# Keyed products and P times V one step further behind the scores in three 16-head attentions

## The reference, cut to what matters

```
scores = einsum('bhqd,bhkd->bhqk', q, k) * scale
scores = where(causal, scores (+ bias in layer 1), -inf)
attn = softmax(scores)
out = einsum('bhqk,bhkd->bhqd', attn, v) @ W_o
```

## Time and profile before

| | |
|---|---|
| median of 3 runs | 2973.53 us |
| lowest, highest | 2969.06, 2974.83 us |
| the profiled execution | 2965.65 us, its span 2963.8 us |
| PE busy | 2372.4 us (80%) |
| DVE, ACT, POOL busy | 1467.8 us (50%), 1140.7 us (38%), 637.5 us (22%) |
| granted clock, mean over the span | 0.898 |

### The profile page before, as it was taken

The page is one execution under the profiler, slowest core; times in us unless marked ns, Lnnn a source line. Parts: engine busy times, 40 slices in busy tenths (PEclk is TensorE's granted clock), DMA queues, the critical chain, the costliest instruction groups (busy, mean ns, idle before and its releaser), DMA issues. The chain is left out here.

```text
span 2963.8 us, 54617 instructions
## 1 busy us (share of the span) xinstructions
PE 2372.4 (80%) x19643; PEld 1552.7 (52%) x19644; DVE 1467.8 (50%) x3082; ACT 1140.7 (38%) x1810; POOL 637.5 (22%) x689
## 2 busy tenths in 40 slices
PE   5487999997799999785888458259997768999987
PEld 1133777773267777332555235135553315777764
DVE  4635666635466664445666123166663254554542
ACT  5623554523254444333555212225453421222223
POOL 0204443300344441011100320521110121211100
PEclk8797999998799999887999789579998867999997
DMA  2000000000000000002222311112220013332320
GB/s 106 0 0 1 1 1 0 0 1 0 0 1 1 0 0 1 1 4 61 76 71 61 144 47 35 46 54 67 72 69 2 32 39 96 99 91 91 91 73 29
DMA packets 81244, 115.93 MB, mean 39 GB/s; under 512 B 10352, under 2 KB 67184, under 8 KB 77720
## 3 DMA queue, kind: packets, MB, share of 16 engines
q1 hardware_dynamic: 79024, 109.35, 12.0%
q0 software_dynamic: 2048, 4.20, 0.5%
HBM read 69.57 MB, written 42.86 MB: 38 GB/s over the span
## 5 line engine op out<-in xcount | busy, mean ns | idle before, releaser
L1247 ACT ACTIVATE at_pr<-ps 128x768 f32<-128x768 f32 x384 | 312.1, 813 | 549.6 <-PE ps L1181 549.6
L1286 DVE TENSOR_REDUCE at_m<-ps 128x2 f32<-128x256 f32 x384 | 163.3, 425 | 424.8 <-PE ps L1163 417.7
L1156 PE MATMUL ps<-at_ks,at_qs 40*128 40x128 f32 (+5 forms) x2048 | 213.6, 308 | 79.4 <-DVE at_m L1287 38.4
L1287 DVE TENSOR_REDUCE at_m<-ps 128x2 f32<-128x512 f32 x384 | 262.1, 682 | 0.0
L692 POOL TENSOR_TENSOR la_tc<-la_ta,la_tb 128x512 f32<-128x512 f32 x128 | 162.3, 1268 | 356.7 <-DVE la_tb L958 356.7
L1175 PE MATMUL ps<-at_qs,at_ks 41*128 41x256 f32 (+5 forms) x2048 | 198.9, 293 | 41.0 <-DMA at_qs<-at_ml 24.1
L709 PE MATMUL ps<-w_l0f,la_hs 128*128 128x512 f32 x256 | 153.8, 686 | 54.9 <-POOL la_hs L674 37.0
L859 ACT ACTIVATE la_pr<-ps 128x640 f32<-128x640 f32 x128 | 90.3, 705 | 267.7 <-PE ps L761 267.4
L1175 PEld LDWEIGHTS ps<-at_qs,at_ks 41*128 41x128 f32 (+2 forms) x2048 | 142.7, 145 | 84.6 <-ACT at_pr L1247 33.5
L1156 PEld LDWEIGHTS ps<-at_ks,at_qs 40*128 40x128 f32 (+2 forms) x2048 | 100.4, 145 | 164.3 <-DVE at_m L1287 66.1
L1196 PE MATMUL ps<-at_pr,at_v 128*32 128x256 f32 (+1 forms) x3072 | 173.3, 337 | 10.5 <-issue 10.1
(11 more groups left out here) (309 smaller groups left out, 5009.7 us busy)
## 6 DMA issues: line engine op xcount, KB each, us to landing
scratch_latent<-at_parts SPq DMA_DIRECT2D x32, 640.0 KB, 4.3
at_qs<-scratch_latent SPq DMA_DIRECT2D x32, 320.0 KB
at_ks<-scratch_latent SPq DMA_DIRECT2D x32, 320.0 KB
scratch_alibi<-at_parts SPq DMA_DIRECT2D x32, 192.0 KB, 2.3
at_ks<-scratch_alibi SPq DMA_DIRECT2D x192, 32.0 KB
scratch_rope<-at_parts SPq DMA_DIRECT2D x32, 192.0 KB, 2.3
at_ks<-scratch_rope SPq DMA_DIRECT2D x192, 32.0 KB
moe_weights<-in_moe SPq DMA_DIRECT2D x1, 4096.0 KB
```

The costliest lines, as they stand in the source:

```text
L1156: nc.tensor.matmul(o[:, cols:cols + keys], q[:, block_q:block_q + P], kk[:, 0:keys], start=(cols == 0), stop=False, skip_group_check=True)
L1247: nc.scalar.activation(pr[:, p % RING, :, :], ps[:, 6:8, 0:384], ACT.Exp, scale=scale).then_inc(s.at_prob, 1)
L1286: nc.vector.tensor_reduce(m2[:, r, 0, x:16:8], ps[:, m:m + 2, 0:128], AX.X, ALU.max, negate=True)
L1287: nc.vector.tensor_reduce(m2[:, r, 1, x:16:8], ps[:, m:m + 2, 128:384], AX.X, ALU.max, negate=True).then_inc(s.at_max, 1)
```

## The change

Two constants grow by one. `values` moves from even to odd steps, as its lag is now odd. The raw copy's step was worked out from the lag, as 6; it would have become 7 and is now written as 6, the step after `values` of pairs 6 and 7 (step 5).

```
-KEY_LAG, VALUE_LAG, VALUE_ROW, RING = 4, 6, 2, 4
+KEY_LAG, VALUE_LAG, VALUE_ROW, RING = 5, 7, 2, 4
...
-                    if x % 2 == 0:
+                    if x % 2 == 1:
                         row = 3 + (x < VALUE_LAG)
                         if live(i, row):
                             values(i - row, (n - row) % slots, (x - VALUE_LAG) % HP)
...
-                    if live(i, 4) and x == (VALUE_LAG + 8) % HP:
+                    if live(i, 4) and x == 6:
                         act.wait_ge(s.at_attended, HP * (b - 3))
```

## The result

Over 18 runs each the kernel after has a median of 2977.16 us (2968.97 to 2989.09), the kernel before 2964.91 us (2949.75 to 2974.83). The ratio is 1.0048, 95% interval [1.0032, 1.0064]: slower by 0.5%, some 14 us (the medians differ by 12.3), where 2968.2 against 2973.53, 0.2% faster, was forecast. The profiled execution of after took 2979.28 us, 13.6 more than that of before.

A forecast was written before the change was run, and what follows sets the result against it. The prediction took the chain of 18 stack loads to bind both bf16 attentions after the change. Its terms, +5.3 − 5.0 − 3.2 − 2.4 = −5.3 us, taken off the median of 2973.53, gave 2968.2 us, range 2959 to 2978.

The forecast's parts named there:

- the load chain takes over both bf16 attentions: First and second attention: the later-released stack loads set the row at 16.8 us; the forecast itself, chance 0.60.
- The row of 16.82 us: Both bf16 attentions: first load 8.77 us into the row plus a chain of 8.05 gives a 16.82 us row.
- Step 4 at 7.87: Bf16 attentions: by summed TensorE steps, step 4 starts 7.87 us after the row's first scores.
- the hold-up that the forecast named: Second attention: VectorE's store of step 2 may hold `product` by up to 0.1 us, +1.2 us at most.
- 1.84 us of landing: Bf16 attentions: the next row's scores start 1.84 us after the last stack load is issued.
- What makes some rows longer lies ahead of the new wait and is absorbed by it: First attention: against the 16.47 us average the row grows only 0.35 us; against the undisturbed 16.29, 0.53.
- Ends of both: Rows 16 and 17 and the drain of both bf16 attentions: sum −3.2 us, bounds 0 and −4.
- Third attention, "−2.4": Third attention: full rows −4.3, fill −1.2, rows 16 and 17 +0.6, drain +2.5; together −2.4 us.
- C: Bf16 attentions: loads land later or step 4 comes later; at a 17.4 us period +8 us, 2981; chance 0.15.
- −5.6 for the rest: Ends of both bf16 attentions and the third attention: −5.6 us beside the rows of the bf16 attentions.
- D: Period 16.8 us, but the third attention gives nothing and the ends cancel: about 0, 2974 us; chance 0.18.
- B: Bf16 attentions: loads do not bind, rows take 15.7 and 16.0 us: −28 us, 2945; chance 0.07.

The follow-up runs named there:

- experiment 1: Kernel before with only the stack loads released one keyed product later, nothing moved on TensorE: ratio 1.0095 to the kernel before.
- experiment 2: Changed kernel with the keyed products' lag back at 4, so only `values` is one step later: ratio 0.9934 to the kernel before.
- Experiment 6: Changed kernel with the third attention's 21 turns written out in place of the loop: ratio 0.9980 to the kernel before.
- experiment 7: Changed kernel with `turn_back` doing its two transposes three times in the third attention: one execution, 2980.62 us.
- experiment 5: Kernel before with the change in the two bf16 attentions only, third attention as before: ratio 0.9999 to the kernel before.
- experiment 8: Kernel before with `values` one step later in the two bf16 attentions only, keyed products and third attention as before: ratio 0.9929 to the kernel before.
- experiment 4: Changed kernel with 12 stack loads for 18, repeated `Ks` blocks read by one load with a repeating source: ratio 1.0343 to the kernel before.

## Why the prediction was wrong

*What bounds the kernel; the load chain takes over both bf16 attentions:* right. Both wait for the stacks in each row, the waits for the maxima are gone, and experiments 1 and 2 put cost and gain where the chain says. SyncE's issue took 6.21 us as before, the step from keyed masks to first load 0.48 (0.47 forecast).

*The row of 16.82 us* is the first step that failed, as a sum with three terms too small: undisturbed it is 17.15, in the second attention 17.0 to 17.1. (a) "Step 4 at 7.87" was 8.04: everything up to step 3's keyed product was hit within 0.03, then `product` came 0.13 late, the hold-up that the forecast named and left out of the first attention, and its own matmuls took 0.04 more. (b) "1.84 us of landing" was 1.98. (c) 0.02 in rounding and the load's start. Together 0.33. Twelve such rows are 205.8 us in the first attention for the forecast 202.4 (197.1 + 5.3), 3.4 us more, and 205.2 (17.1 each) in the second for 202.4, 2.8 us more.

*"What makes some rows longer lies ahead of the new wait and is absorbed by it"* was wrong the other way round. What lies ahead of step 4's keyed masks delays the loads and lengthens the chain, and the longer waits bring a new disturbance, the half clock. Rows 4 to 15 took another 4.9 us more in the first attention (210.72 for 205.8) and 4.7 in the second (209.93 for 205.2).

*Row 4* has 1.8 and 2.6 us of that, and it shows how. In row 3 of after the keyed products start a step later, at 1396.66 us, so TensorE is done sooner and stands still for the loads that go out directly behind the copies of the maxima; these loads wait for no keyed product. The first scores of row 4 behind that wait, first attention with its keyed masks of step 4, then second attention:

```profile
1403.73 0.50 PE L1156 MATMUL ps<-at_ks,at_qs 54*128 54x128 bf16 x4 [2.24 <-DMA at_ks<-scratch_alibi]
...
1414.16 0.40 PE L1181 MATMUL ps<-cast 128*128 128x128 bf16 x4
```
```profile
2010.34 0.49 PE L1156 MATMUL ps<-at_ks,at_qs 48*128 48x128 bf16 x4 [2.19 <-DMA at_ks<-scratch_rope]
```

Before, this wait was 0.46 us in the first and none in the second. By itself it costs little: row 3 takes 14.04 us for 14.69, and 14.80 for 14.72. But around or behind it lie 6.8 us at half clock in each attention. So the keyed masks of step 4 start 10.43 us into row 4 instead of 8.48, and the next loads, which now wait for them, as much later. The forecast counted row 4 as a row like the others.

*Ends of both, "−3.2"*: −2.8, so the sum held. Its parts did not: row 16, for which −0.7 and −0.9 were forecast, changed by +0.55 and −0.18, and row 17 with the drain by −1.57 and −1.09. Rows 2 and 3, counted as nothing, changed by −0.6 and +0.1.

*Third attention, "−2.4"*: the step algebra was right to 0.01 us in steps 2 to 5 and in the row (28.11 for 28.2), and the loads stayed covered. It holds for eight of the twelve rows 5 to 16. The term that was missing is the ends of the loop: +5.9 over rows 5 to 15 where −4.3 was forecast. Experiment 6 shows that the loop costs it (15.0 us), 2 that moving `values` brings it on, and 7 points to the emptied step 0 as what keeps the clock low behind the gap. That the third attention as a whole is off by only 2.9 us is luck: its fill and its end came out 7.4 us below the forecast, with 5.7 us less at half clock in the fill (29.6 for 35.3) and 10.2 us less in the drain (13.7 for 23.9), which the forecast did not reckon with.

By these terms: 8.3 + 7.5 in rows 4 to 15 of the two attentions, 0.4 at their ends, 2.9 in the third are 19.1 us, the whole of the difference between +13.7 and −5.3. Of these, 6.2 are the three terms of the undisturbed row and 9.6 are the rows that were to be absorbed.

*Rivals.* C, "slower: step 4 comes later or the landing takes longer", is what happened: step 4 came 0.17 later and the landing took 0.14 longer. The undisturbed row is 17.15, but the average period from row 5 to row 16 is 17.44 in the first attention, over the 17.2 that the forecast named as C's sign, and C's prices at 17.4, +12 and +1.6, are near the measured +13.6 and +2.5. Its −5.6 for the rest was −2.3. D, "the third gives nothing", came true for another reason than D named: the loop's ends took what the other rows saved. B's rows, 15.7 and 16.0 from TensorE's own steps, were seen in experiment 2, at 15.87 and 16.33, where the loads are released a step sooner. That the range held the bare number (2977.16 of 2978) is luck too: the kernel before has another median in the runs beside it (2964.91 for 2973.53). As a difference the range reached from −14.5 to +4.5 us, and the change measured some +14. It reached only to one rival at a time; that C and D might come together was not counted.

*What stays open.* The timed parts do not add up to the whole: +14 us for the change, −0.3 us [−7, +7] in the two bf16 attentions alone, −0.6 us [−8, +7] in the third alone. By the profiles the bf16 attentions carry it: the first took 287.8 to 292.7 us in five profiles with the change and 279.6 to 280.7 in four without, the second 295.4 to 300.1 and 291.2 to 295.6. By the timed runs of experiments 5 and 8 their keyed products' step costs about 21 us and their `values` give as much back. One execution of one kernel differs from the next by up to 34 us here, and the total of the third attention alone by up to 13 between kernels that have it alike (488.7 to 501.8), mostly by half clock; what lies outside the three attentions, the same in all versions, took 1888 to 1902 us. So the mechanism is shown in the traces and in experiments 1 and 2; how much of the 14 us each attention bears is not settled by the timed runs. Open too is what sets the moment of the instruction fetch at the loop's end.

## What to carry to other kernels

A lag that grows by one step holds its buffer a step longer: before taking a wait away on the engine, add up the refill chain of that buffer (last reader, issue, landing) and compare it with the row; and try the two halves of such an edit apart, since here one was worth −0.7% and the other took more than that back. An interval that is "absorbed" must lie behind the event that starts the chain; what is ahead of it is added. Do the sum for the fill and for each end of a loop as well as for the undisturbed row, as short steps and gaps there also decide the clock.

## What the hardware showed that was not expected

- At the end of a loop TensorE stood still, waiting for no engine and no DMA of the program, 1.94 to 3.84 us. At each such gap a 16384-byte packet of the instruction queue was moved (0.96 to 1.70 us), and the first matmul came 1.6 to 1.7 us after that packet's end (1.43 once), at 22 gaps of eleven kernels. At the first gap of before the packet began 0.7 us before the last work ended; at that of after it began 0.25 us behind it, as the row's stores started, and took 1.39 instead of 0.96 us.
- The granted clock fell to 0.50 behind 18 of these 22 gaps (1.9 to 3.8 us), for 3.4 to 17.1 us (23.9 once), and in the bf16 attentions around some waits of only 1.2 to 2.8 us, for 3.4 or 6.8 us. How long it lasted differed with the work behind the gap (experiment 7). That 0.50 and 1.00 are the only levels in these profiles agrees with the Trainium skill, "TensorE: Matmul & The Clock Gate", Part 1 on the clock gate.
- Loads with a repeating source took 0.74 to 0.81 us (three repeats) and 0.66 to 0.67 us (two) from start to start, against 0.34 for a plain one, and the scores came 4.36 us behind the last issue, against 1.98 (experiment 4).
